# Three float32r passes with split operands in place of one fp32 product, in the query, key, value and first feed-forward products of a small language-model tower

## What is computed

```python
q = x @ Wq[i] + bq[i]
k = x @ Wk[i] + bk[i]
v = x @ Wv[i] + bv[i]
Q = jax.nn.elu(q) + 1.0
K = jax.nn.elu(k) + 1.0
KV = jnp.einsum('nsh,nsh->nh', K, v, precision='highest')
Ksum = jnp.sum(K, axis=1)
Z = 1.0 / (Q * Ksum[:, None, :] + 1e-06)
V = Q * KV[:, None, :] * Z
a = jax.nn.gelu(V @ Wo[i] + bo[i])
a = jax.nn.gelu(a)
x = _ln(a + residual, ln1_s[i], ln1_b[i])
residual = x
h = jax.nn.gelu(x @ W1[i] + b1[i])
f = jax.nn.gelu(h @ W2[i] + b2[i])
x = _ln(f + residual, ln2_s[i], ln2_b[i])
```

## Time and profile before

| | us |
|---|---|
| runs, median of 3 | 1232.18 (1231.64 to 2161.32) |
| profiled execution, its span | 1236.4 |
| embedding and step 0, in that execution | 0 to 70.95 |
| step 1 | 70.95 to 120.03 |
| steps 2 to 13, twelve steps | 43.05 each |
| steps 14 and 15 | up to 721.0, where the tail begins |

### The profile page before, as it was taken

The page is one execution under the profiler, slowest core; times in us unless marked ns, Lnnn a source line. Parts: engine busy times, 40 slices in busy tenths (PEclk is TensorE's granted clock), DMA queues, the critical chain, the costliest instruction groups (busy, mean ns, idle before and its releaser), DMA issues. The chain is left out here.

```text
span 1236.4 us, 16294 instructions
## 1 busy us (share of the span) xinstructions
PE 1099.6 (89%) x4826; PEld 719.3 (58%) x4826; DVE 757.8 (61%) x2088; ACT 580.1 (47%) x973; POOL 316.1 (26%) x316
## 2 busy tenths in 40 slices
PE   4899999999999999999999989868988778787882
PEld 3556557656665765676576566635545445476661
DVE  2577665785777578567758763657787765332221
ACT  2572563464356446535644634545656542033341
POOL 6030010011001001100301010332006573557775
PEclk9999999999999999999999989879989778899896
DMA  5300110220022211102430000377522215279897
GB/s 129 117 1 1 48 73 21 82 94 27 21 72 68 68 60 47 59 33 83 151 141 1 18 1 2 79 161 127 105 53 94 71 56 214 62 169 186 170 232 138
DMA packets 58452, 103.05 MB, mean 83 GB/s; under 512 B 10858, under 2 KB 38214, under 8 KB 58123
## 3 DMA queue, kind: packets, MB, share of 16 engines
q1 hardware_dynamic: 39227, 59.29, 17.9%
q0 software_dynamic: 19152, 42.92, 13.5%
HBM read 58.59 MB, written 53.00 MB: 90 GB/s over the span
## 5 line engine op out<-in xcount | busy, mean ns | idle before, releaser
L563 PE MATMUL b_ring<-left 128*128 128x256 f32 x960 | 212.1, 379 | 0.0
L553 PE MATMUL b_ring<-right,left 128*128 128x512 f32 x480 | 208.4, 592 | 0.0
L563 PEld LDWEIGHTS b_ring<-left 128*128 128x128 f32 x960 | 181.4, 190 | 25.0 <-issue 1.0
L1104 POOL TENSOR_TENSOR b_rstd<-b_veps,b_mhalf 128x4 f32<-128x4 f32 x31 | 36.7, 1185 | 560.1 <-DVE b_veps L1178 560.1
L553 PE MATMUL b_ring<-XT,b_wqkv 128*128 128x512 f32 x384 | 170.1, 592 | 0.0
L553 PEld LDWEIGHTS b_ring<-right,left 128*128 128x128 f32 x480 | 91.2, 190 | 114.8 <-issue 103.0
L853 ACT ACTIVATE left<-b_ring,b_cur 128x512 f32<-128x512 f32 x128 | 88.0, 687 | 65.4 <-PE b_ring L553 44.3
L553 PEld LDWEIGHTS b_ring<-XT,b_wqkv 128*128 128x128 f32 x384 | 71.6, 190 | 77.6 <-issue 76.9
L1290 DVE RECIPROCAL b_mixing<-b_mixing 128x1024 f32<-128x1024 f32 x16 | 104.8, 6553 | 0.5
L2085 ACT ACTIVATE a_ET<-a_pB 128x512 f32<-128x512 f32 x128 | 74.2, 595 | 44.5 <-PE a_pB L1835 43.2
L1769 POOL DMA_INDIRECT xe<-m_row,m_idx x84 | 82.7, 984 | 46.2 <-issue 28.2
(11 more groups left out here) (336 smaller groups left out, 1871.3 us busy)
## 6 DMA issues: line engine op xcount, KB each, us to landing
xe<-b_nil POOLq DMA_DIRECT2D x16, 1284.0 KB, 5.9
a_ET<-xe SPq DMA_DIRECT2D x32, 321.0 KB, 4.0
left<-in_w SPq DMA_DIRECT2D x8, 1024.0 KB, 5.4
x_wt<-in_wexp SPq DMA_DIRECT2D x16, 384.0 KB, 4.7
b_wqkv<-in_wqkv SPq DMA_DIRECT2D x4, 768.0 KB, 4.6
b_rows<-in_rows SPq DMA_DIRECT2D x8, 384.0 KB, 5.0
right<-qparts SPq DMA_DIRECT2D x16, 192.0 KB, 4.9
left<-qparts SPq DMA_DIRECT2D x16, 192.0 KB, 5.0
```

What stands on the lines that cost most here:

```text
L553: last = pe.matmul(bank[:, :], lhsT(k), rhs(k), start=(k == 0), stop=(k == n_k - 1))
L563: last = pe.matmul(bank[:, j * D:(j + 1) * D], src[:, k, tile], weights[:, k, :], start=(k == 0), stop=(k == n_k - 1))
L1104: pool.tensor_tensor(rstd[:, :], veps[:, :], mhalf[:, :], ALU.pow).then_inc(s_rs, 1)
```

## The change

The rounded type float32r (`F32R`) is laid over the same buffers (`rounded_name` gives a second name at an address). Each operand of the q, k, v and first feed-forward products becomes two: a high part, written as float32r, and a low part, the difference between the number and its high part. A product is then high x high + low weight x high + high weight x low, three float32r matmuls per half of the contraction, in one PSUM bank. The activations' high part is the ACT copy out of PSUM (one instruction over both banks in place of two); their low part is a DVE subtraction, PSUM minus high part, for `XT` (`x_lowered`, after the mixing) and for `X1T` (`x1_low`, inside the second norm). The weights' high part is a DVE copy (`wqkv_high` at the end of every fourth step, `w1_high` after the first step of a block), their low part a POOL subtraction in place over the loaded weights (`wqkv_low`, `w1_low`). The second feed-forward, the output projection and all later phases keep fp32. `eqk` now lies on `nqk`, `junk` goes away, `xf` moves; five semaphores of a later phase are merged into two.

```diff
-                def product(n_k, lhsT, rhs):
-                    bank = bank_free()
-                    for k in range(n_k):
-                        last = pe.matmul(bank[:, :], lhsT(k), rhs(k), start=(k == 0), stop=(k == n_k - 1))
+                def high_products(bank, high, low, x):
+                    for k in range(KD):
+                        pe.matmul(bank[:, :], high(k), x(k), start=(k == 0), stop=False)
+                        pe.matmul(bank[:, :], low(k), x(k), start=False, stop=False)
+
+                def low_products(bank, high, lows):
+                    for k in range(KD):
+                        last = pe.matmul(bank[:, :], high(k), lows(k), start=False, stop=(k == KD - 1))
                     last.then_inc(s_full, 1)
...
                 if s % NC == 0:
-                    pe.wait_ge(s_wqkv, loaded)
-                if s >= NC:
-                    pe.wait_ge(s_x, NC * l + s - NC + 1)
-                else:
-                    pe.wait_ge(s_xc, s + 1)
+                    pe.wait_ge(s_wl, 2 * (l + s // NC) + 1)
+                pe.wait_ge(s_x, NC * l + s + 1)
                 qkv(0)
...
                     if (s - 1) % NC == 0:
-                        pe.wait_ge(s_w1, loaded1)
+                        pe.wait_ge(s_wl, 2 * (l + (s - 1) // NC) + 2)
+                    pe.wait_ge(s_x1h, NC * l + s)
+                    banks = [up_high(f) for f in range(2)]
                     pe.wait_ge(s_x1, NC * l + s)
-                    for f in range(KF):
-                        product(KD, lambda k: w1[:, k, f * P:(f + 1) * P], lambda k: X1T[:, k, :])
+                    for f in range(2):
+                        up_low(f, banks[f])
+                    for f in range(2, KF):
+                        up_low(f, up_high(f))
...
             def x1_copied(item):
                 act.wait_ge(s_r1, item + 1)
-                for m in range(KD):
-                    last = act.activation(X1T[:, m, :], pR[m][:, :], ACT.Copy)
-                last.then_inc(s_x1, 1)
+                act.activation(X1H, pRR[:, :, :], ACT.Copy).then_inc(s_x1h, 1)
...
+            def w1_low(b):
+                pool.wait_ge(s_wh, 2 * b + 2)
+                pool.tensor_tensor(w1_lo, w1, w1_hi.bitcast(F32), ALU.subtract).then_inc(s_wl, 1)
...
                 deviations(s2, link)
+                if between:
+                    between()
                 gained(s2, rows2[:, 1, :], link)
...
+            def x1_low(s, l):
+                dve.wait_ge(s_x1h, NC * l + s)
+                dve.tensor_tensor(X1L, pRR[:, :, :], X1H.bitcast(F32), ALU.subtract).then_inc(s_x1, 1)
+
+            def x_lowered(s, l):
+                dve.wait_ge(s_xh, NC * l + s + NC - 1)
+                c = (s - 2) % NC
+                dve.tensor_tensor(x_low[s % 2], pRR[:, :, :], XH[:, :, c * CH:(c + 1) * CH].bitcast(F32), ALU.subtract).then_inc(s_x, 1)
...
                 if s == 1:
+                    embedded_low(2)
+                    x1_low(s, l)
                     embedding_norm(3)
...
+                elif ln2(s):
+                    x_lowered(s, l)
                 if s == 0:
+                    embedded_low(1)
                     embedding_norm(2)
+                if s == 1:
+                    embedded_low(3)
+                if s % NC == NC - 1 and s < ITEMS - 1:
+                    wqkv_high(l + (s + 1) // NC)
...
+                if s % NC == 0:
+                    w1_high(l + s // NC)
```

More of the change, by code:

```diff
@@ L6 @@
 F32 = mybir.dt.float32
+F32R = mybir.dt.float32r
 BF16 = mybir.dt.bfloat16
@@ L152, in words, with rounded_name @@
     return places[:, :, :, :].rearrange("p n h t -> p (n h t)").bitcast(F32)
+def rounded_name(nc, name, numbers):
+    with nc.sbuf_tensor(name, [P, numbers], F32R) as cells:
+        return cells
 def grid(cells, rows):
@@ L209, in core_phase @@
         nqk = mixing[:, 0:2048].rearrange(four, j=2, m=KD)
-        eqk = mixing[:, 2048:4096].rearrange(four, j=2, m=KD)
+        eqk = nqk
         rqk = mixing[:, 4096:6144].rearrange(four, j=2, m=KD)
@@ L263, in core_phase @@
         pN = pb("b_pN", [P, TPC, D])
-        pR = [pb(f"b_pR{i}", [P, CH]) for i in range(KD)]
+        pRR = pb("b_pR", [P, KD, CH])
+        pR = [pRR[:, k, :] for k in range(KD)]
         pT = pN[:, 0:2, :].rearrange("p a b -> p (a b)")
@@ L283, in core_phase @@
         s_xt = sem("e_xn_transposed")
-        s_xc = sem("e_xT_ready")
         s_wqkv = sem("b_wqkv_loaded")
@@ L630, in late_w1 @@
                     pe.wait_ge(s_free, A_END + f - 1)
+                cols = slice(f * P, (f + 1) * P)
                 for k in range(KD):
-                    last = pe.matmul(bank[:, :], w1[:, k, f * P:(f + 1) * P], X1T[:, k, :], start=(k == 0), stop=(k == KD - 1))
+                    pe.matmul(bank[:, :], w1_hi[:, k, cols], X1H[:, k, :], start=(k == 0), stop=False)
+                    pe.matmul(bank[:, :], w1_lo[:, k, cols], X1H[:, k, :], start=False, stop=False)
+                    last = pe.matmul(bank[:, :], w1_hi[:, k, cols], X1L[:, k, :], start=False, stop=(k == KD - 1))
                 last.then_inc(s_full, 1)
@@ L811, in xT_copied @@
                 act.wait_ge(s_xt, c + 1)
-                for k in range(KD):
-                    last = act.activation(XT[:, k, c * CH:(c + 1) * CH], pR[k][:, :], ACT.Copy)
-                last.then_inc(s_xc, 1)
+                act.activation(XH[:, :, c * CH:(c + 1) * CH], pRR[:, :, :], ACT.Copy).then_inc(s_xh, 1)
             def h_copied(t):
@@ L929, in body @@
                     c = (s - 2) % NC
-                    for m in range(KD):
-                        last = act.activation(XT[:, m, c * CH:(c + 1) * CH], pR[m][:, :], ACT.Copy)
-                    last.then_inc(s_x, 1)
+                    act.activation(XH[:, :, c * CH:(c + 1) * CH], pRR[:, :, :], ACT.Copy).then_inc(s_xh, 1)
                 if s == ITEMS - 1:
@@ L950, in columns_copied @@
                 for k in range(KD):
-                    last = act.activation(XT[:, k, c * CH:(c + 1) * CH], pR[k][:, :], ACT.Copy)
+                    last = act.activation(XT[:, k, c * CH:(c + 1) * CH], pR[k], ACT.Copy)
                 last.then_inc(s_fx, 1)
@@ L984, in query_columns_copied @@
                 for k in range(KD):
-                    last = act.activation(xT[c][:, k, :], pR[k][:, :], ACT.Copy)
+                    last = act.activation(xT[c][:, k, :], pR[k], ACT.Copy)
                 last.then_inc(s_fx, 1)
@@ L1121, in _ @@
             embedding_rstd(2)
+            w1_low(0)
             pool.wait_ge(s_ve, NC)
@@ L1129, in _ @@
                 pool.tensor_tensor(hc, hc, lnb[:, :].unsqueeze(1).to_broadcast([P, TPC, D]), ALU.add).then_inc(s_lb, 1)
[L1130 to L1133, removed]
+            with pool.Fori(0, LOOPS) as l:
+                for i in range(NC):
+                    for j in range(2):
+                        block_rstd(2 * NC * l + 2 * i + j + 2)
+                    tables_prepared(NC * l + i)
+                    if (i + STEPS_BEFORE) % NC == NC - 1:
+                        wqkv_low(l + 1)
+                    if (i + STEPS_BEFORE) % NC == 0:
+                        w1_low(l + 1)
             for i in range(LAST, ITEMS):
@@ L1270, in body @@
                     n += 1
-                    second_norm(s, l, chain.link, n)
+                    second_norm(s, l, chain.link, n, lambda: x1_low(s, l))
                 dve.wait_ge(s_qkv, NC * l + s + 1)
@@ L1334, in _ @@
             embedding_norm(0)
+            wqkv_high(0)
+            embedded_low(0)
             embedding_norm(1)
@@ L1362, in _ @@
             second_sum(ITEMS, 0)
+            x1_low(ITEMS, 0)
             squared(0)
```

94 lines of the change are left out of this document (69 added, 25 removed).

## The result

| | before | after |
|---|---|---|
| runs, median | 1236.86 us (1231.64 to 2161.32) | 1216.92 us (1208.82 to 1220.46) |
| ratio, 95% interval | | 0.984 (0.980 to 0.987) |
| profiled execution, span | 1236.4 | 1214.4 |

A forecast was written before the change was run, and what follows sets the result against it. DVE's chain replaces PE as bound, step 43.05 to 40.21 us: 34.2 (steps 2 to 13) + 7.2 (14, 15) - 8 (start) - 0.6 = 32.8 us off the 1236.4 span; median 1199 us, range 1188 to 1240 (0.80).

The forecast's parts named there:

- first term: DVE chain, step start to ACT's last query/key bank: 24 passes x 0.216 = 5.18 us, ACT 0.2 later: 5.38.
- PE's waits: In each regular step PE waits about 0.7 us for `X1H`, 1.0 for `x1_low`, 1.3 for the mixing.
- the pace of a pass: Float32r pass of 512 columns: 216 ns, so a q, k, v or feed-forward matmul falls from 858 to 648 ns.
- The estimate of 427 ns: Rival of four-byte columns at half pace, there 429 ns a pass: step 55.1 us, about 1424 us; chance 0.11.
- the three steps with `w1_low`: POOL's `w1_low` makes DVE's `first_sum` wait some 3.8 us; `x1r` then late, costing 0.2 us, three times.
- step 1: Line 1294 (mixing, before `wo`) 7.5 us late from `w1_low(0)`, `embedded_low(2)`, `x1_low` waits; +8 for both start steps.
- The tail: After the steps: `x1_low` holds DVE up some 4 us, but DVE waited 6.08 there for PE: 0.
- that last term: Final step of the sum: median lies 4.2 us below the execution's span, so span 1203.6 becomes 1199 us.
- the case that had 0.58: Whole kernel measured faster, under 1207.5 us (2%, 24.6 us, less): chance 0.58.
- the one that had 0.25: Whole kernel measured the same, its difference within 2% (24.6 us): chance 0.25.
- the slow rivals: Changed products: half-pace columns, 429 ns a pass, about 1424 us, chance 0.11; weight loads not hidden, 323 ns, 1282, 0.06.
- The clock's rival: New PE waits lower the clock in most steps, or passes take 250 to 280 ns: 1209 to 1235 us; chance 0.13.

The follow-up runs named there:

- no_x1_low: Changed kernel without the DVE subtraction `x1_low` in the steps, the third feed-forward pass reading X1H again: 1194.2 us, ratio 0.967 to the kernel before.
- gelu_mid: Changed kernel with ACT's gelu `f_made` moved from before the first value bank to after the second query bank: 1200.6 us, ratio 0.973 to the kernel before.
- joined: Changed kernel with `f_made` earlier, the W1 split earlier and POOL's last-bias additions held until step 1's mixing is done: 1177.9 us, ratio 0.952 to the kernel before.
- w1_early: Changed kernel with W1 split earlier: `w1_high` right behind `x_lowered`, and for the first block ahead of the steps: 1204.7 us, ratio 0.976 to the kernel before.
- adds_late: Changed kernel with POOL's four additions of the last bias to h held back until step 1's mixing is done: 1204.8 us, ratio 0.973 to the kernel before.
- before_moves: Kernel before the change, with only `f_made` moved behind the second query bank and POOL's additions held until step 1's mixing: 1230.7 us, ratio 0.996.
- v_halves: Changed kernel with the value products' two k = 1 passes of 512 columns split into four of 256: steps stayed at 40.6 us; one run.

## Why the prediction was right, and where it was off

**Right: DVE takes over.** The chain came out nearly as worked out, but for its first term: from the start of a step to the last query and key bank on ACT, 298.73 - 292.82 = 5.91, forecast 5.38. From the last query and key bank on ACT to `second_sum`: 300.55 - 298.73 = 1.82, forecast 1.82. To mixing: 7.77, forecast 7.88. Mixing to `wo`: 14.86, forecast 14.77. `wo` to the next step: 10.27, forecast 10.36. `no_x1_low` and `gelu_mid` shorten that chain in two ways, and the step follows. PE's waits were forecast at 0.7, 1.0 and 1.3 us; two came, of 0.82 and 0.74.

**Off: the pace of a pass.** 216 ns were taken; passes that follow each other without a wait are 228 to 241 ns apart, 232 on average (79 of the 84 in a step of `joined`). The fp32 record of 256 columns, on which the 216 rested, was the right neighbour but not the same thing. The query and key passes of that step are 230 ns apart: 24 x 0.014 = 0.34 of the 0.53 us by which that first term was forecast too short. The first pass of a step, 0.42 us in place of 0.23, makes the other 0.19. The regular step exceeds 40.21 by 0.42: over eleven steps 4.6 us, the largest term of the miss. The estimate of 427 ns, made from the moving-operand figure of the Trainium skill ("SBUF — State Buffer", A bandwidth-pool intuition that's wrong), is refuted by 232; of the two pages that were weighed the one on four passes for true fp32 ("FP8 and Floating Point Precision", TensorE Precision Notes) came much nearer. PE alone needs 38.8 us (busy time in `joined`), not 37.2, so 1.8 us of PE's gain was lost to DVE, not 3.0.

**Off: the three steps with `w1_low`.** The collision was foreseen and sized (3.8 us against a measured 3.4), but what is late next was followed along `x1r` alone and put at 0.2 us. The bias addition behind the first norm also frees a bank for PE; it was 1.26 us a step, 3.2 us of the miss. `w1_early` shows it by taking it away.

**Off: step 1.** Line 1376 was forecast 7.5 us late and was 9.4 late (115.51 against 106.15). `first_sum` cost 3.7 in place of 2.55 (it ended at 78.97, not at 76.6 + 1.2), the wait for copy and `x1_low` 4.4 in place of 3.8, `embedded_low(2)` its 1.2. The second collision, 6.2 us in the third embedding norm, was read as given because it was there before; `adds_late` shows that it was worth as much as all that the change added to step 1. That line 1376 was 1.9 us later than forecast did not show in the sum, and that was luck: the loss to the lower clock, which was to double from 1.8 us, stayed at 1.6 (42.2 us to the `wo` of step 2, where a regular step has 40.6). The 1.5 us that the start lost against the forecast lie in step 0: its `wo` was to start 1.3 us earlier and started 0.2 later (67.5 before, 67.7 after). In this execution the clock was 0.50 there from 48.7 to 52.1 us, behind a wait of PE of 2.94 us. In the six profiled runs of changed kernels whose clock stayed at 1.00 in step 0, its `wo` starts at 65.3 to 65.7 us; in `before_moves`, where the clock stayed at 1.00 too, at 66.9. That is 1.2 to 1.6 us less, so the gain that was forecast is there.

**The tail** was put at 0 and gave 0.8, but nothing can be told there: `v_halves` repeats the changed kernel from step 0 to 15 to within 0.1 us and has a tail of 521.0 in place of 526.6. Over all the executions profiled here the tail runs from 519.7 to 527.8.

**The sum.** 4.6 (pace), 3.2 (steps with `w1_low`), 1.5 (start), 0.6 (steps 13 to 15) and 0.8 (tail) make 10.7 of the 10.8 us of the span. By the spans the ratio went from the forecast 0.973 to 0.982. The medians add to that. The prediction took 4.2 us off its span because the median run before lay that much below the profiled execution's span, but those were two different executions: in one and the same, the time is 1.6 us above the span (1216.03 and 1214.4). So that last term had the wrong sign, and 5.8 of the 17.9 us between 1199 and 1216.9 are its. The measured ratio of 0.984 left the case that had 0.58 for the one that had 0.25. The rivals did not come: a pass of 232 ns is far from the 280 of the slow rivals (the step would be 43.05 again at 24.0 / 84 = 286), weight loads are hidden, the clock is 1.00 in the steps from 2 on. The clock's rival gave the right amount, 1209 to 1235, by luck and for the wrong reason, apart from step 1, where the lower clock did cost.

## What to carry to other kernels

When the engine that bounds a loop is made faster, work out the next longest chain with every queue position on it, for it decides what arrives; then look whether an instruction of that chain can be issued earlier, which costs nothing and was worth as much here as two thirds of the change's own gain. Collisions and waits that the old bound had hidden come out at full price: of each, ask not only which result is late next but also which buffer comes free late.

## What the hardware showed that was not expected

The pace of a float32r pass does not scale in full with TensorE's clock. In the tail the clock is 0.50 from 704.1 to 717.7 us, where PE has waited 3.37 us ahead of 702.71 and then 2.37 us more, and the passes are 427 ns apart; at a clock of 1.00 they are 232 apart, a factor of 1.84. PE's timeline there:

```profile
712.57 0.79 PE L677 MATMUL b_ring<-right_rounded,b_mixing_rounded 128*128 128x512 f32 x1 [2.37 <-DVE parts_rounded L1332]
713.16 0.63 PE L678 MATMUL b_ring<-right_rounded,left_rounded 128*128 128x512 f32 x1
713.58 0.63 PE L679 MATMUL b_ring<-parts_rounded,b_mixing_rounded 128*128 128x512 f32 x1
714.01 0.63 PE L677 MATMUL b_ring<-right_rounded,b_mixing_rounded 128*128 128x512 f32 x1
```

512 columns at 1.2 GHz take 427 ns, which comes to one column a cycle; at 2.4 GHz they would be 213, and the pass takes 19 more. By the estimate from `v_halves` some 9 of these go with each instruction; what the others are was not settled, nor why neither part is seen at 1.2 GHz.
